# Order of steps in a mixer and expert kernel: TensorE's second half of a group, two VectorE steps and one ScalarE step moved

## The reference

```
scores = (C . B^T) * decay * dt          Y_intra = scores . X
S      = (B * w)^T . X                   H_next  = dlast * H + S
Y_inter = (C * exp(cum)) . H             y = Y_intra + Y_inter + D_skip * X
out = rmsnorm(y * silu(z)) . out_proj
```

## Time and profile before

| | us |
|---|---|
| median of three runs | 2582.05 |
| the profiled execution's own time | 2583.38 |
| its span, first to last instruction | 2581.7 |
| TensorE busy | 2504.3 |
| VectorE busy | 2150.2 |
| ScalarE busy | 1820.8 |
| GpSimd busy | 2084.7 |

### The profile page before, as it was taken

How to read it: one execution, slowest core, us unless ns; L and a number is a source line. 1 busy time by engine, 2 the same in 40 slices (tenths; PEclk the granted TensorE clock), 3 DMA queues, 4 the chain that set the end, 5 groups by cost and what they waited for, 6 DMA issues and landing times. The chain is left out here.

```text
span 2581.7 us, 59964 instructions
## 1 busy us (share of the span) xinstructions
PE 2504.3 (97%) x19384; PEld 1982.3 (77%) x19384; DVE 2150.2 (83%) x5557; ACT 1820.8 (71%) x3745; POOL 2084.7 (81%) x2939
## 2 busy tenths in 40 slices
PE   5899999999999999999999999999999999999987
PEld 4678877778777778777778777778778778778776
DVE  5678888888888888888888888888888888888887
ACT  4567777777777777777767777777777777776754
POOL 4478888888888888888888888888888888888875
PEclk8999999999999999999999999999999999999999
DMA  4000000000000000000000000000000000000000
GB/s 146 9 10 14 6 8 12 12 12 12 4 8 12 12 12 12 4 8 12 12 12 12 4 8 12 12 12 8 8 8 12 12 12 4 12 8 12 9 5 9
DMA packets 28861, 34.34 MB, mean 13 GB/s; under 512 B 2704, under 2 KB 27280, under 8 KB 28240
## 3 DMA queue, kind: packets, MB, share of 16 engines
q1 hardware_dynamic: 28816, 33.77, 4.2%
HBM read 25.37 MB, written 8.39 MB: 13 GB/s over the span
## 5 line engine op out<-in xcount | busy, mean ns | idle before, releaser
L1220 DVE SCALAR_TENSOR_TENSOR acc<-bank,cw,acc 128x253 f32<-128x253 f32 x1920 | 770.1, 471 | 99.4 <-ACT acc L840 97.8
L1619 PE MATMUL bank<-hT,w_in 128*128 128x256 f32 x2560 | 617.4, 385 | 13.6 <-DVE acc L1220 11.0
L1619 PEld LDWEIGHTS bank<-hT,w_in 128*128 128x128 f32 x2560 | 479.4, 191 | 129.4 <-issue 36.8
L628 POOL TENSOR_TENSOR Em<-ee 128x1024 f32<-128x1024 f32 x256 | 491.7, 1932 | 97.5 <-DVE rden L1356 94.9
L1376 DVE SCALAR_TENSOR_TENSOR Em<-Em,p 128x1024 f32<-128x1024 f32 x256 | 356.9, 1424 | 101.6 <-POOL Em L628 101.6
L643 POOL TENSOR_TENSOR W<-W,Em 128x1024 f32<-128x1024 f32 x124 | 295.0, 2379 | 54.1 <-ACT Em L975 45.9
L975 ACT ACTIVATE Em<-Em,rden 128x1024 f32<-128x1024 f32 x256 | 290.2, 1146 | 54.5 <-DVE Em L1386 52.0
L840 ACT ACTIVATE acc<-bank,cb,cw 128x253 f32<-128x253 f32 x640 | 323.6, 559 | 0.0
L1386 DVE TENSOR_TENSOR Em<-Em,products 128x1024 f32<-128x1024 f32 x248 | 297.3, 1210 | 0.0
L1820 PE MATMUL bank<-h2T,w_up 128*128 128x256 f32 x1024 | 245.6, 383 | 2.7 <-ACT hid L953 2.1
L1854 PE MATMUL bank<-w_ue,WT 128*128 128x256 f32 x1024 | 236.3, 384 | 2.0 <-ACT WT L985 2.0
(11 more groups left out here) (209 smaller groups left out, 4847.3 us busy)
## 6 DMA issues: line engine op xcount, KB each, us to landing
x_in<-x_dram SPq DMA_DIRECT2D x32, 256.0 KB, 2.7
x_res<-x_dram SPq DMA_DIRECT2D x32, 256.0 KB, 2.7
out_dram<-f SPq DMA_DIRECT2D x32, 256.0 KB, 2.2
w_in<-in_wT_dram SPq DMA_DIRECT2D x1, 1544.0 KB, 8.9
w_in<-in_wT_dram SPq DMA_DIRECT2D x1, 1024.0 KB, 5.4
w_up<-upT_dram SPq DMA_DIRECT2D x1, 1024.0 KB, 13.6
w_de<-down_eT_dram SPq DMA_DIRECT2D x1, 1024.0 KB, 15.6
w_down<-downT_dram SPq DMA_DIRECT2D x1, 1024.0 KB, 17.6
```

The lines of the kernel that those rows point to most:

```text
L628: nc.gpsimd.tensor_tensor(Em[:, k], bc(ee[:, k, 0:XD], 2, KEYS), bc(ee[:, k, XD:XD + KEYS], 1, XD), ALU.mult).then_inc(E_done.sem, 1)
L1220: ins = V.scalar_tensor_tensor(acc[:, r, a, TAPS - 1:], ps[:, a * TOK + k:(a + 1) * TOK - TAPS + 1 + k], cw[:, t, k:k + 1], acc[:, r, a, T ...
L1619: last = mm(ring[j % 2][:, a * TOK:(a + 1) * TOK], w_in[:, k, at:at + P], hT[:, k, :], start=k == 0, stop=k == DK - 1)
```

## The change

ScalarE: `silu_head(g)` stands ahead of `mixer_norm(n)`. VectorE: `ffn_times(f, 0, 3)` and `mixer_conv(g, 0)` stand ahead of `tail_sum(e)`; `mixer_conv(g, 9)` stands ahead of `mixer_parts(g)`. TensorE: `ffn_out(f, 1)` ahead of `mixer_rows(g, 0)`; `mixer_B(g, 0)` ahead of `mixer_X(g, 1)`; `mixer_Yn` is split in three, `yb_free` (its first waits), `mixer_skip` and `mixer_Yn`, with the same products; in the second chunk `mixer_yT(g, 0)` comes between skip and Yn, and `mixer_S(g, 1)` directly behind Yn; `mixer_out(g, 0)` comes ahead of `mixer_yT(g, 1)`, and `mixer_out(g, 1)` moves behind `mixer_pair(g + 1, 0)` of the next pass (for the last group, ahead of `ending`). No instruction is added or removed and no transfer is touched.

```diff
@@ ScalarE, do_group
                     silu(g, PAIRS - 2)
+                if a:
+                    silu_head(g)
                 if n is not None:
                     mixer_norm(n, e)
-                if a:
-                    silu_head(g)
@@ VectorE, do_group
                     mixer_step(e, 1)
+                if c:
+                    ffn_times(f, 0, 3)
+                if a:
+                    mixer_conv(g, 0)
+                if b:
                     tail_sum(e)
-                if c:
-                    ffn_times(f, 0, 3)
-                if a:
-                    mixer_conv(g, 0)
-                if b:
                     tail_residual(e)
...
-                if g is not None:
+                if a:
+                    mixer_conv(g, 9)
                     mixer_parts(g)
-                if a:
-                    mixer_conv(g, 9)
@@ TensorE
-            def mixer_Yn(g, c, e, n):
+            def yb_free(g, c, e, n):
...
+            def mixer_Yn(g, c):
+            def mixer_skip(g, c):
@@ TensorE, do_group
                     mixer_pair(g, 0)
+                if b:
+                    mixer_out(e, 1)
                 if c:
                     ffn_down(f, 0)
...
+                if c:
+                    ffn_out(f, 1)
                 if a:
                     mixer_rows(g, 0, f)
-                if c:
-                    ffn_out(f, 1)
-                if a:
                     mixer_X(g, 0)
...
                 if a:
+                    mixer_B(g, 0)
                     mixer_X(g, 1)
-                    mixer_B(g, 0)
                     mixer_scores(g, 0)
                     mixer_S(g, 0)
                     mixer_rows(g, 1, f)
-                    mixer_Yn(g, 0, e, n)
+                    yb_free(g, 0, e, n)
+                    mixer_Yn(g, 0)
+                    mixer_skip(g, 0)
                     mixer_B(g, 1)
                     mixer_Yi(g, 1)
                     mixer_scores(g, 1)
-                    mixer_Yn(g, 1, e, n)
+                    yb_free(g, 1, e, n)
+                    mixer_skip(g, 1)
                     mixer_yT(g, 0)
+                    mixer_Yn(g, 1)
                     mixer_S(g, 1)
+                    mixer_out(g, 0)
                     mixer_yT(g, 1)
-                    mixer_out(g, 0)
-                    mixer_out(g, 1)
```

More of the change, by code:

```diff
@@ L1425, in do_group @@
                     mixer_step(e, 1)
-                    tail_sum(e)
                 if c:
@@ L1431, in do_group @@
                 if b:
+                    tail_sum(e)
                     tail_residual(e)
@@ L1465, in do_group @@
                     mixer_stats(n)
-                if g is not None:
-                    mixer_parts(g)
                 if a:
                     mixer_conv(g, 9)
+                    mixer_parts(g)
                 if a and not later(g):
@@ L1745, in mixer_Yn @@
                                   stop=c > 0 and h == HEADS - 1)
-                if c == 0:
[L1747 to L1752, removed]
+                if c:
+                    last.then_inc(Yn_ps.sem, 1)
+            def mixer_skip(g, c):
+                pe.wait_ge(skips, INNER // P)
+                for i in range(INNER // P):
+                    last = mm(yb[:, i * P:(i + 1) * P], xbcT[:, i, c * P:(c + 1) * P],
+                              skip[:, 2 * i:2 * i + 2, :].rearrange("p h d -> p (h d)"), start=c > 0 and i == 0,
+                              stop=c == 0 and i == INNER // P - 1)
+                if c == 0:
+                    last.then_inc(Yn_ps.sem, 1)
             def mixer_yT(g, c):
@@ L1919, in do_group @@
                     ffn_up(e, 3)
-                if a:
-                    mixer_rows(g, 0, f)
                 if c:
@@ L1924, in do_group @@
                 if a:
+                    mixer_rows(g, 0, f)
                     mixer_X(g, 0)
@@ L1958, in _ @@
             do_group(NG - 1, NG - 2, NG - 3, None)
+            mixer_out(NG - 1, 1)
             def ffn_sum(e, c, h, before):
```

## The result

The change makes the kernel slower by a fifth of a per cent: 2588.61 us median (2586.73 to 2590.59, 11 runs) against 2582.95 (2581.70 to 2585.34, 11 runs) for the kernel before on the same chip (the 2582.05 of the opening is the median of three of these eleven), a ratio of 1.0021 with a 95% interval of 1.0014 to 1.0029. That is +5.7 us on the medians; the profiled spans say +5.0 (2586.7 against 2581.7). Forecast were +8.8.

What follows compares the result with a forecast made beforehand. TensorE, busy for 97% of the span, was taken as the bound, tied to VectorE and GpSimd. 30 passes x (0.20 + 0.05) = +7.5, plus 1.3 at the start, gave +8.8 us on 2582.05: 2590.9, range 2577 to 2603.

Steps and rivals of the forecast that it cites:

- rival of no change: Pair 3's full slack of 0.37, yT costing 0.43 and parts meeting nothing leave passes within 0.06 us: 2585.2; chance 0.25.
- Tie 1: S(g, 0) waits for GpSimd's `Xw`, ending a chain without slack; TensorE's savings ahead become waiting: gain 0 a pass.
- rival that `Xw` moves by itself: Faster case: `Xw` comes earlier through another rhythm, S(g, 0) follows the scores at once: 2565.7 us; chance 0.16.
- signs of being right: Expected profile: S(g, 0) waits 0.8 to 1 us, passes 78.0 to 78.1, pair 3 28.0 us behind S(g, 0).
- Parts: VectorE's five `mixer_parts` instructions now run beside GpSimd's `mixer_head` and collide, delaying `ffn_choose`: +0.05 us a pass, bounds 0 and +0.4.
- rival of full blocks: Each of five parts instructions waits for a GpSimd head instruction to end, 0.8 us a pass: 2613; chance 0.09.
- Tie 2: Later Yn(g, 1) delays gate, GpSimd's run, `rs`, residual, convolution 1 and pair 3: +0.20 us a pass, bounds +0.06 and +0.41.
- slack of pair 3: Time convolution 1 may slip before pair 3's matmul is late: 0.18 or 0.37 us by reading, 0.28 taken.
- TensorE's own gain: Half of the output projection no longer waits, some 0.2 us; TensorE only reaches pair 3 earlier and waits longer.
- Sum and convolution 0: VectorE's sum moves to right ahead of `tail_residual`, covered by GpSimd: cost 0 a pass, bounds 0 and +0.3.
- The start: Group 1 lacks group f's cover, so pair 3 waits longer for convolution 1: +1.3 us, bounds 0 and +3.
- The ending: Last group's projection: first half falls into idle time, second leaves TensorE cold; taken 0, bounds -3.0 and +3.0 us.

Runs made afterwards that it cites:

- the early edits alone: Kernel before with only the head's Silu, convolution 9, rows and B moved as in the change: 2582.09 us, ratio 0.9996.
- root back and convolution 1 first: Kernel after with `ffn_root(f)` behind `mixer_decay(g, 0)`, `ffn_norm(f)` behind `mixer_move(g, 1)`, and `mixer_conv(g, 1)` ahead of `tail_residual`: 2579.64 us, ratio 0.9987.

## Why the prediction was right, and where its terms were off

*The sign and the two ties were right; that the loss is clear of noise is in part luck.* The ties were the right frame: neither chain changed a link, and what TensorE saved turned into waits for `Xw` and for convolution 1. The sum said +8.8 us, the medians +5.7, the spans +5.0. But the conditions of the rival of no change came true (a slack of 0.37, a move of yT not above 0.43, nothing for the parts), and its 2585.2 allowed for 0.06 us a pass. What lifts the loss from 0.02 to 0.12 us a pass is a term that my sum did not have. So the sum came near with two terms too large and one absent.

*Tie 1: 0 a pass. Right.* 18.42 us against 18.43, and the early edits alone leave the pass at 77.80. The rival that `Xw` moves by itself is refuted by the same run. I gave the new wait as 0.7 to 1.1 us; it is 0.8 at the weight load and 0.61 at the matmul. The pass of 77.94 us and pair 3 at 27.79 lie below the 78.0 to 78.1 and the 28.0 that I gave as signs of being right.

*Parts: +0.05 forecast, 0 measured.* They lasted 0.22, 0.34, 0.22, 0.36 and 0.41 us, 0.09 in all above their times elsewhere, which fits in VectorE's 0.17 us of idling ahead of `ffn_choose`. That begins 5.70 us behind `ffn_up(e, 2)` in both kernels. I let five meetings of 0.07 happen where fewer than two did, though the kernel's own row for L1206 was the right price for one. My price of a full block came from a cast, which has one input; the three of the five that have two lay 0, 0.02 and 0.07 us above their means. The rival of full blocks asked for 0.8 us a pass and is refuted for these short instructions.

*Tie 2: +0.20 forecast, +0.12 measured, from three terms of which two were off and one was missing.* Yn moved by 0.39, not 0.48, and less than my lower bound of 0.43: I took all but 0.1 of yT's 0.59 us to go ahead of Yn, but it came to stand between products of its own shape and Yn, so skip took 0.89 instead of 1.04 and yT 0.53. The slack of pair 3 was the full 0.37, not the middle of my two readings: its matmul begins 0.05 us after the convolution's last row ends, with the weight load in the same moment, so the load does not need to be complete in the way I assumed. 0.39 - 0.37 = 0.02, and 27.79 - 27.77 = 0.02. The missing term is the start-up of pair 3 behind its wait, 1.83 us for a block in place of 1.73, which I counted nowhere: +0.10, most of the loss. By the slack and the move alone the rival of no change would have been the better one. (The 2586.6 that I gave for all short ends does not follow from my bounds either: 2582.05 + 30 x 0.06, with nothing at the start, is 2583.9.)

*TensorE's own gain: some 0.2 us forecast, 0.31 measured,* and for another reason. I expected the split projection to wait less; by itself it costs 0.05 us. The gain is by all rows the changes of tile shape, which I had put at "about 0.1, paid in any order". They are not paid in any order: two fewer, 0.34 us. It did not matter to the sum, since tie 2 took it all, but it is why undoing yT's move did not bring the old pass back.

*Sum and convolution 0: 0 a pass. Right,* as the run with the sum back shows. *The start: +1.3 forecast, +1.6 in the profiles,* which is luck as well. Of the 1.6 us 0.8 lie ahead of S of group 0 (72.53 against 71.70), where I had put the early edits at nothing. The run with the sum back puts the sum's own part at up to 225.41 - 222.06 = 3.4 us in the profiles and 1.7 in the medians; I had not seen that two short waits would merge into one of 5.33 us, behind which the granted clock falls. *The ending: 0 forecast,* 0.1 measured: the first half of the last projection did fall into the idle stretch, and the next step did pay for the second (eight instructions in 4.40 us, before 3.43).

Not tried: the kernel after with a faster GpSimd run ahead of `rs`, so which part of tie 2 is cheapest to shorten stays open. Why S of group 0 differs by up to 2.3 us between profiles of the same order is open as well.

## What to carry to other kernels

A reordering that removes waits on the busiest engine gains only if the engines that feed it come earlier too; follow each chain from the step that is moved later to the next place where the busy engine reads its result, and compare its delay with the slack there. Undoing one edit does not measure it when another chain is as long: the same move of a convolution gained 0.44 us a pass behind this change and nothing without it. When a tie is loosened, read the next row with a wait before adding another edit; here two moves that had gained 0.44 and 0.32 us a pass alone gained 0.33 together, until the third wait, on ScalarE, was moved too; then all three made 1.12 us a pass, 31 us from the changed kernel.

## What was not expected of the hardware

- A change of TensorE's tile shape between `128*128` and `128*64` costs time: 3.78 us up to the projection for the same four blocks that took 3.44 in another order, 0.34 us for two changes more.
- A matmul block that starts up behind a wait of 0.16 us takes 0.10 us longer to the next block (1.83 against 1.73), as much as one behind a change of shape: the half projection behind S takes 1.83 too (1249.68 to 1251.51 in the kernel after).
- Long instructions of VectorE and GpSimd do hold each other up where short ones hardly do. In the run with root back and convolution 1 first, the mask, which reads two inputs in SBUF, lasts 2.90 us while GpSimd's second Em and Xdt run, against 1.28 in the same pass of the kernel after. The Trainium skill ("SBUF — State Buffer", SBUF: two separate sides) describes a port pair held for a whole instruction; the 2.90 us agree with it, the 0.09 us of the parts are far less than a full block of each.

```profile
1230.84 2.90 DVE L1377 SCALAR_TENSOR_TENSOR Em<-Em,p 128x1024 f32<-128x1024 f32 x1 [0.84 <-POOL Em L628]
```

```profile
1228.82 3.84 POOL L628 TENSOR_TENSOR Em<-ee 128x1024 f32<-128x1024 f32 x2 [2.95 <-issue]
1232.72 1.92 POOL L537 TENSOR_TENSOR Xdt<-Xt,dts 128x512 f32<-128x512 f32 x1
```
